# A gated recurrence with the expert products beside it: two of three matmuls cut to the current step, the expert work cut into halves, biases as bfloat16 parts over the full array

## The reference, cut to what matters

```python
def step(h, inp):                     # 256 steps, h is [8, 128]
    xr_t, xz_t, xn_t = inp            # x W_ir + b_ir, x W_iz + b_iz, x W_in + b_in
    r = sigmoid(xr_t + h @ W_hr)
    z = sigmoid(xz_t + h @ W_hz)
    n = tanh(xn_t + r * (h @ W_hn + b_hn))
    h_new = (1.0 - z) * n + z * h
...
for e in range(8):                    # tokens are the 2048 states
    y = relu(tokens @ W1[e] + b1[e]) @ W2[e] + b2[e]
    out = out + where(final_e == e, y, 0)   # final_e: arg max of the router, or 0 over capacity
```

## Time and profile before

| | us |
|---|---|
| timed runs | 1562.0, 1564.18, 1564.52 (median 1564.18) |
| profiled execution, its own time | 1565.08 |
| span of its trace, first to last instruction | 1563.3 |
| mean granted TensorE clock over the span | 0.956 of full speed |

### The profile page before, as it was taken

One profiled execution on the slowest core, in us unless ns is written; L12 is line 12 of the kernel. 1 busy time (PEld: TensorE's weight loads), 2 busy tenths in 40 slices (PEclk: granted clock), 3 DMA queues, 4 the chain that ended last, 5 costly groups with the idle time before them and its releaser, 6 DMA issues. The chain is left out here.

```text
span 1563.3 us, 29989 instructions
## 1 busy us (share of the span) xinstructions
PE 1440.9 (92%) x10908; PEld 1119.0 (72%) x10909; DVE 720.6 (46%) x2677; ACT 646.6 (41%) x2429; POOL 132.0 (8%) x216
## 2 busy tenths in 40 slices
PE   7999988999989999999999998699999999848995
PEld 4333323777779999999999998278888888735663
DVE  3576764554533444444444443833333333573223
ACT  2322213655613455555545553034444444532442
POOL 4000000000000000000000000110000000225661
PEclk9899989999999999999999999599999999978998
DMA  5000000000030000000000000010000000001113
GB/s 159 1 0 0 1 0 1 0 1 1 0 109 1 2 2 1 2 1 2 1 1 2 2 1 1 6 44 22 22 22 22 22 16 2 8 21 34 43 42 96
DMA packets 27788, 27.92 MB, mean 18 GB/s; under 512 B 2358, under 2 KB 22299, under 8 KB 27515
## 3 DMA queue, kind: packets, MB, share of 16 engines
q1 hardware_dynamic: 21034, 16.70, 3.6%
q0 software_dynamic: 2496, 5.12, 1.1%
q10 hardware_dynamic: 4112, 4.19, 0.9%
HBM read 21.35 MB, written 4.65 MB: 17 GB/s over the span
## 5 line engine op out<-in xcount | busy, mean ns | idle before, releaser
L1669 PE MATMUL spare<-identb 128*128 128x128 bf16 x2996 | 211.5, 221 | 0.0
L1669 PEld LDWEIGHTS spare<-identb 128*128 128x128 bf16 x2996 | 195.0, 104 | 4.5
L1158 ACT ACTIVATE ghid<-gh_ps,cols 128x128 f32<-128x128 f32 x512 | 144.2, 365 | 12.9 <-PE gh_ps L1059 12.7
L1223 DVE TENSOR_TENSOR_SCAN narg<-rz,pre_n 128x16 f32<-128x16 f32 x256 | 48.0, 187 | 220.2 <-PE pre_n L1120 219.0
L1059 PE MATMUL gh_ps<-hist,w 128*128 128x128 f32 x1024 | 137.4, 275 | 0.6 <-ACT ghid L1158 0.6
L1068 PE MATMUL gy_ps<-w2e,ghid 128*128 128x128 f32 x1024 | 136.8, 277 | 0.8 <-DVE g_diff L1204 0.2
L1068 PEld LDWEIGHTS gy_ps<-w2e,ghid 128*128 128x128 f32 x1024 | 124.4, 191 | 3.1 <-issue 3.1
L1059 PEld LDWEIGHTS gh_ps<-hist,w 128*128 128x128 f32 x1024 | 125.8, 188 | 0.8 <-DVE hist L1231 0.8
L1144 ACT ACTIVATE rz<-pre_r 128x8 f32<-128x8 f32 x256 | 45.6, 178 | 182.0 <-PE pre_r L1120 179.4
L1120 PE MATMUL pre_r<-hist,gru_w 128*128 128x128 f32 x512 | 118.2, 312 | 0.8 <-DVE hist L1231 0.5
L1729 DVE TENSOR_TENSOR_SCAN targ<-gates,pairs 128x16 f32<-128x16 f32 x256 | 49.2, 192 | 143.3 <-ACT gates L1679 143.3
(11 more groups left out here) (411 smaller groups left out, 2514.6 us busy)
## 6 DMA issues: line engine op xcount, KB each, us to landing
w<-in_L_ffn_W SPq DMA_DIRECT2D x1, 2048.0 KB, 10.4
raw<-in_L_ffn_wg SPq DMA_DIRECT2D x8, 256.0 KB, 3.1
raw<-in_L_ffn_wu SPq DMA_DIRECT2D x8, 256.0 KB, 2.9
raw<-in_L_ffn_wd SPq DMA_DIRECT2D x8, 256.0 KB, 2.6
wqkv<-in_L_attn_Wqkv SPq DMA_DIRECT2D x1, 1536.0 KB, 6.2
mrow<-mt SPq DMA_DIRECT2D x8, 128.0 KB, 1.8
y_top<-yrow SPq DMA_DIRECT2D x4, 256.0 KB, 5.3
y_next<-yrow ACTq DMA_DIRECT2D x4, 256.0 KB, 6.1
```

The lines of the kernel that those rows point to most:

```text
L1158: nc.scalar.activation(hid[v % 2][:, f, :], h_ps[:, f, :], ACT.Relu, bias=n.cols[:, at:at + 1]).then_inc(h_done, 1)
L1223: V.tensor_tensor_scan(narg[p][:, :], rz[p][:, 0:16], n_slot(s), 0.0, ALU.mult, ALU.add).then_inc(narg_done, 1)
L1669: nc.tensor.matmul(spare[:, 0:P], n.identb[:, :], n.identb[:, :], start=True, stop=True)
```

## The change

- `r` and `n` take only the 8 columns of the current step as the moving operand; `z` keeps 128.
- The four bias rows and b2 are split on GpSimd into three bfloat16 parts each, at partitions 0, 32 and 64 of `bias_parts`, which is zero elsewhere; the bias matmul has 128 rows of bfloat16 weights and a square of ones. The split runs at the start of `linear_attention`, in 18 small GpSimd operations; for it the rows are loaded three times (10 DMAs more on SP's queue), and GpSimd fills two more tiles at the start of the kernel.
- Jobs are cut into halves: each step issues two blocks of `hidden(u)` and two of `output(u-1)`; ScalarE makes two relus in each step, in the same step as their hidden products. Two blocks of PSUM hold the hidden products instead of four.
- The sigmoid of z is taken with scale -1, so `fresh` is 1 - z at once; `mix` becomes (fresh - 1) h in one VectorE operation and the tanh is taken with scale -1. `keepz` is gone.
- The router's pieces use spare columns of the idle `pre_r` bank and stand at other steps; logits take 8 columns instead of 128, the one-hot is 128 columns wide with three copies, and its transposition and its product with b2 use the full array.
- The 16 logits matmuls after the last step are issued together before the remaining jobs, and the remaining 16 halves follow with one half a step.

```diff
@@ inputs, g bias @@
-                        lhsT, rhs = n.gru_b[:, i - 3, :], n.ones_row[:, :]
+                        lhsT, rhs = n.bias_parts[:, i - 3, :], n.ones_b[:, :]
...
-                def hidden(v):
-                    g, e = divmod(v, E)
-                    if v:
-                        pe.wait_ge(h_done, NF * v)
-                    for f in range(NF):
-                        mm = nc.tensor.matmul(h_ps[:, f, :], w1[:, e, P * f:P * f + P], tokens(g), start=True, stop=True)
+                def hidden(u):
+                    v, half = divmod(u, 2)
+                    grp, e = divmod(v, E)
+                    if u == 0:
+                        pe.wait_ge(n.load_experts, 32)
+                    else:
+                        pe.wait_ge(h_done, 2 * u)
+                    for f in (2 * half, 2 * half + 1):
+                        mm = nc.tensor.matmul(h_ps[:, f % 2, :], w1[:, e, P * f:P * f + P], tokens(grp), start=True, stop=True)
...
+                    if s - G < HALVES:
+                        hidden(s - G)
+                    if 0 <= s - G - 1 < HALVES:
+                        output(s - G - 1)
...
-                        for out, i, ready in ((r_out, 3, r_pre), (n_out, 5, n_pre), (z_out, 4, z_pre)):
-                            nc.tensor.matmul(out, n.gru_w[:, i, :], h, start=False, stop=True,
+                        for out, i, rhs, ready in ((gate_slot(pre_r, s), 3, now, r_pre), (first(n_slot(s)), 5, now, n_pre),
+                                                   (z_out, 4, h, z_pre)):
+                            nc.tensor.matmul(out, n.gru_w[:, i, :], rhs, start=False, stop=True,
...
                     elif s == T:
                         pe.wait_ge(state, T + 1)
+                        for m in range(NBLK):
+                            b, half = divmod(m, SEG)
...
-                        V.tensor_scalar(second(keepz[p][:, :]), z, -1.0, 1.0, ALU.mult, ALU.add).then_inc(z_used, 1)
-                        V.tensor_tensor(second(mix[p][:, :]), z, second(at_step(s)), ALU.mult).then_inc(z_used, 1)
-                        dve.wait_ge(z_used, 2 * s + 2)
+                        V.scalar_tensor_tensor(second(mix[p][:, :]), second(fresh[p][:, :]), 1.0, second(at_step(s)),
+                                               ALU.subtract, ALU.mult).then_inc(mixed, 1)
+                        dve.wait_ge(mixed, s + 1)
```

More of the change, by code:

```diff
@@ L981, in gru_scan @@
         pre_n = [ps(f"pre_n{i}", [P, 512]) for i in range(2)]
[L982 to L985, removed]
+        h_ps = ps("gh_ps", [P, 4, P])[:, 0:2, :]
+        y_ps = ps("gy_ps", [P, 512])[:, 0:P]
+        reset = [sb(f"reset{i}", [P, 16]) for i in range(2)]
         narg = [sb(f"narg{i}", [P, 16]) for i in range(2)]
-        keepz = [sb(f"keepz{i}", [P, 16]) for i in range(2)]
+        fresh = [sb(f"fresh{i}", [P, 16]) for i in range(2)]
         mix = [sb(f"mix{i}", [P, 16]) for i in range(2)]
@@ L1076, in work @@
                         return
[L1077 to L1089, removed]
@@ L1105, in _ @@
+                    if k == 5 and grp < GROUPS:
+                        pe.wait_ge(choice_kept, grp + 1)
+                        pe.wait_ge(kept, 2 * grp)
+                        nc.tensor.matmul(spare(grp, 2), n.bias_parts[:, 4, :], choiceT[:, :], start=True, stop=True).then_inc(bias_in, 1)
                 for i in range(7):
@@ L1111, in _ @@
                         h = second(hist[:, 16 * s:16 * (s + G)]).rearrange("p (s b) -> p s b", b=B)
-                        at = 16 * (s % G)
                         at8 = B * (s % G)
-                        r_out, z_out = (pre[s // G % 2][:, at8:at8 + P].rearrange("p (s b) -> p s b", b=B) for pre in (pre_r, pre_z))
-                        n_out = first(pre_n[s // G % 2][:, at:at + 16 * G]).rearrange("p (s b) -> p s b", b=B)
+                        z_out = pre_z[s // G % 2][:, at8:at8 + P].rearrange("p (s b) -> p s b", b=B)
+                        now = second(at_step(s))
                         if s == 24:
@@ L1233, in _ @@
-                    g, k = jobs_at(s)
-                    if g < 0:
+                        V.tensor_tensor_scan(at_step(s + 1), fresh[p][:, :], mix[p][:, :], 0.0,
+                                             ALU.mult, ALU.subtract).then_inc(state, 1)
+                    if s < G:
                         continue
-                    if k == 4 and g:
-                        keep(g - 1)
-                    if k == 2 and g < GROUPS:
-                        choose(g, 0)
-                        choose(g, 1)
@@ L1250, in _ @@
[L1250 removed]
+                    grp, k = divmod(s - G, G)
+                    if k == 3 and grp:
+                        keep(grp - 1)
+                    if k == 4 and grp < GROUPS:
+                        dve.wait_ge(choice_in, grp + 1)
+                        V.tensor_copy(choiceT[:, :], spare(grp, 2)).then_inc(choice_kept, 1)
+                    if k == 5 and grp < GROUPS:
+                        dve.wait_ge(bias_in, grp + 1)
+                        V.tensor_copy(diffT[:, P * grp:P * grp + P], spare(grp, 2)).then_inc(bias_kept, 1)
@@ L1251, in _ @@
+                    v = (s - G) // 2 - 1
                     if k % 2 == 0 and 0 <= v < JOBS:
                         add(v)
-                    if s == T + NBLK + 1:
+                    if k == 0 and grp < GROUPS:
+                        choose(grp, 0)
+                    if k == 1 and grp < GROUPS:
+                        for i in range(1, 4):
+                            choose(grp, i)
+                    if s == T + 1:
                         dve.wait_ge(all_logits, 1)
```

157 lines of the change are left out of this document (87 added, 70 removed).

## The result

The changed kernel takes 1527.9 us (median of 4 runs, 1527.29 to 1528.85), the kernel before 1564.35 beside it: a ratio of 0.976, 95% interval 0.974 to 0.979. It is faster by 36 us. The forecast was 1530 us, range 1508 to 1556. The profiled execution took 1528.5 us, with a span of 1526.7.

A forecast was written before the change was run, and what follows sets the result against it. A plain recurrence step was taken as bound by the chain through z's gate, 0.14 us above TensorE's need. Recurrence -55.9, clock +15.5, start -1.5, tail +7.5 make -34.4 on 1565.1: 1530 us, range 1508 to 1556.

The forecast's parts named there:

- The time a plain step takes: Recurrence: one VectorE operation fewer brings a plain step from 1.72 to 1.63 us.
- The dear steps: Recurrence: the five bias and b2 steps in each 16 fall from 2.19 to 1.63 us, 2.8 us a group.
- -55.9: Whole recurrence: 429.9 us against 485.8, if the clock is up throughout.
- The step with the transpositions: Recurrence, router's pieces: three transpositions of one pass each in one step make it 1.91 us.
- Short columns: Recurrence, r and n: 8 columns save TensorE under 0.01 us together; r's sooner sigmoid is worth nothing.
- The rival with cheap short passes: Recurrence: short passes cost about 25 ns, steps end near 1.3 us, about 75 us less: 1455 us; chance 0.02.
- The clock at the start: Start of the recurrence: short passes delay the clock's rise to steps 9 to 11, +15.5 us.
- rival 1: Start of the recurrence: clock rises in the second step as before, only 2 of 15.5 us stay: 1516 us; chance 0.27.
- rival 2: Recurrence: the clock never rises, steps of 3.1 us with extras, +304 us: about 1882 us; chance 0.16.
- Behind the last step: Tail: logits 6.5 us, then 16 halves of 1.41 us, +5.4, and +2 for a falling clock; 7.5 in the sum.
- rival 3: Recurrence: ScalarE's relus become the last, a slip of 0.1 us a step gives +24: 1554 us; chance 0.10.
- What I had at zero: Routing, gate stage and what lies behind it: no change, 0 us.

The follow-up runs named there:

- e6: The changed kernel with 1 - z and z h as two VectorE operations again; median 1534.16 us without one outlying run, ratio 0.983.
- e1: The changed kernel with r and n over 128 columns again; 1526.01 us, ratio 0.975.
- e2: The changed kernel with the four GRU biases as one row of float32 weights again, b2 left on the full array; 1565.92 us, ratio 1.002.
- e4: The changed kernel with hidden products of odd halves behind the last step written into an idle bank; 1519.02 us, ratio 0.968.
- e5: The changed kernel with the logits products behind the last step issued one behind each of the last halves; 1515.26 us, ratio 0.968.
- e8: The changed kernel with odd halves' hidden products in an idle bank and logits products between the last halves; 1516.41 us, ratio 0.967.
- e12: The changed kernel itself run once more for a second trace; 1525.07 us, ratio 0.975.
- e15: The changed kernel with each bfloat16 bias product followed by a second one of the same weights and zeros; 1527.78 us, ratio 0.977.
- e3: The changed kernel with 8 columns for z's product too; 1896.68 us, ratio 1.212.
- e11: The changed kernel with z at 8 columns too and six bfloat16 filler products in each plain step from step 17 on; 1957.25 us, ratio 1.252.

## Why the prediction was right, and where not

**The time a plain step takes** was right: 1.63 to 1.64 us, by the end of one VectorE operation. It started 0.21 behind the start of z's sigmoid, in place of 1 - z and mix, and e6 gives it 10 us. The sigmoid of z, the new state and the next product's load stand at 0.98, 1.39 and 1.63, each where the forecast had it.

**The dear steps** were right in kind and mis-sized by a little. They left 2.19 for 1.68, not for 1.63. The step that failed is "each is now one bfloat16 pass beside full-array neighbours, at most half of 0.113": it is 0.11, the price of a weight load of 128 columns, and 14 loads and this one are 1.68. The Trainium skill (TensorE: Matmul & The Clock Gate, section "LDWEIGHTS (loading the stationary operand)") gives 107 ns for 128 columns whatever moves, and names no type of data; the trace agrees with 0.11. The forecast had used that section for float32 alone. It is 3 us of the 5.4 by which the recurrence missed -55.9; the rest is the step with b2's product, at 1.68 as well (0.8 us), the first interval of 2.43 (0.8), and some 0.01 in plain steps. The step with the transpositions took 2.02 and not 1.91, but the one behind it 1.52 and not 1.63. The printed terms of the recurrence add up to 429.5, not 429.9, which changes nothing.

**Short columns** were right: nothing (e1). The rival with cheap short passes (1455 us) didn't come.

**The clock at the start** was wrong, and it was the term that set the forecast apart from its first rival: +15.5 us was forecast and 0.8 came, in the first interval. That is the condition of rival 1 (1516 us). The measured time is 12 us above that rival's, by some 3 us in the recurrence and the 8 in later stages, and so it came near the forecast for reasons that the forecast did not give. What I missed stands in "four of six recurrence passes move only 8 columns", which counts the recurrence's own passes and not the four bias products ahead of step 0. In four traces, all with z over 128 columns, only the one with one-row biases and short r and n stayed low:

| r, n | biases | clock up at |
|---|---|---|
| 128 columns | one row (before) | 459.9 |
| 128 columns | bfloat16 (e1) | 454.4 |
| 8 columns | bfloat16 (changed) | 456.0 |
| 8 columns | one row (e2) | 485.5 |

The six further traces with z over 128 columns, short r and n and bfloat16 biases (e4, e5, e6, e8, e12, e15) have the clock up before the second narg too. So the mechanism exists, with the rise at steps 9 to 11 that I had put, and in the changed kernel the full-array biases are what keeps it away. It must be by the four products ahead of step 0, since up to step 11 nothing else on TensorE differs between the changed kernel and e2: the next group's biases stand at steps 12 to 15. Whether they do it by the rows that they use or by being over in 0.56 us and not in 2.00 isn't shown, and the late rise was traced once; but none of e2's ten timed runs is below 1561.7 us, where an early rise would give some 1552.

**The clock that never rises** (rival 2, 1882 us, chance 0.16) was one product away: e3 took 1897 us.

**Behind the last step** was right in mechanism and size: +8.1 for +7.4, which the sum takes as 7.5. The logits took 7.07 us for 6.5, a half 1.44 for 1.41, and the clock fell over the short products as feared. e5 shows that nearly all of it was avoidable.

**ScalarE** (rival 3) was as near as forecast and cost nothing. The mark that I had named for it is there: r's sigmoid starts as the second relu ends. Counted from the weight load, the relus start at 1.43 as forecast, and r's sigmoid comes 0.43 behind its load where 0.42 was due. The price of the rival was wrong: in e1 the sigmoid comes 0.54 behind its load (711.36 to 711.90), and the step is 1.65. So a slip of 0.1 there costs 0.01 and not 0.1, since the z gate is last.

**What I had at zero**: the gate stage took 6.1 us more in one execution and 0.7 less in another, the routing 0.8 more in the first and nothing in the second. A term for the scatter of the clock in later stages, some 7 us wide, would have been right.

## What to carry to other kernels

In this kernel a float32 product with one row of weights made a step 0.5 us longer than a bfloat16 one over the full array, so put biases into a full array; here that alone was 32 us of 36, at the price of a few lines. Before columns are cut from a product whose price is the weight load, ask what they do for the clock: here the cut on r and n wins nothing, and the same cut on z costs 369 us. Work that is taken out of a pipeline's gaps and put into a block of its own behind it (the logits) is paid in full; put it back into the gaps.

## What the runs showed of the hardware

The granted clock isn't told by TensorE's busy time: 0.50 for 800 us at 99.9% busy (e3), and 0.50 for 864 us with bfloat16 filler in between (e11). From the start of a one-row product, two float32 passes, to that of r's next product it is 0.41 (901.12 to 901.53), from a bfloat16 product over the full array, one pass, 0.06 (698.31 to 698.37). The Trainium skill (TensorE: Matmul & The Clock Gate, section "Why this matters for your kernels") says that a single product with 32 rows takes the time of one with 128. No run here has 32 rows; with 1 row among 128-row neighbours a step is 0.38 us longer than with a full-array float32 product (2.18 and 1.80, e2). One kernel's gate stage differed by 6.8 us between two executions, by where in it the clock fell.
